# Edge convolutions of a graph network: TensorE picks the rows of 5 of 17 tiles with one-hot matrices, GpSimd gathers the other 12

## The reference

```python
def _egnn_conv(x, src, dst, edge_attr, W_msg, W_edge, W_root, b):
    msg = x[src] @ W_msg + edge_attr @ W_edge
    agg = jax.ops.segment_max(msg, dst, num_segments=x.shape[0])
    agg = jnp.where(jnp.isneginf(agg), 0.0, agg)
    return agg + x @ W_root + b
c1 = leaky_relu(_egnn_conv(X, ...1)); c2 = leaky_relu(_egnn_conv(c1, ...2))
x = _layernorm(x + c2)
```

## Time and profile before

| what | us |
|---|---|
| median of 3 runs | 3147.15 (3136.76 to 3154.84) |
| the profiled execution's own time | 3183.81 |
| its span, first to last instruction | 3181.8 |
| loop of layer 0, first sum to last maximum | 1910.6 to 2473.7 |
| loop of layer 1, to its last maximum | 2550.0 to 3119.4 |

### The profile page before, as it was taken

The page is one execution under the profiler, slowest core; times in us unless marked ns, Lnnn a source line. Parts: engine busy times, 40 slices in busy tenths (PEclk is TensorE's granted clock), DMA queues, the critical chain, the costliest instruction groups (busy, mean ns, idle before and its releaser), DMA issues. The chain is left out here.

```text
span 3181.8 us, 47118 instructions
## 1 busy us (share of the span) xinstructions
PE 2077.3 (65%) x15259; PEld 1621.9 (51%) x15259; DVE 1566.5 (49%) x5813; ACT 268.0 (8%) x521; POOL 1421.2 (45%) x1251
## 2 busy tenths in 40 slices
PE   2397566999999999968557954444444544444442
PEld 1132114999999999958453443333333433333331
DVE  7699897555555555554450043333333333333336
ACT  3175441000000000001100010000000000000000
POOL 0100005888888884000000026666666466666663
PEclk9855556999999999969688965555555555555555
DMA  0391001222222221000009612222222222222221
GB/s 24 119 408 66 1 1 1 3 2 3 3 3 2 3 3 2 2 4 1 4 1 361 242 40 75 77 82 77 76 80 74 59 75 75 79 77 81 76 76 51
DMA packets 139880, 197.83 MB, mean 62 GB/s; under 512 B 91361, under 2 KB 92929, under 8 KB 136082
## 3 DMA queue, kind: packets, MB, share of 16 engines
q0 software_dynamic: 83472, 42.24, 11.4%
q1 hardware_dynamic: 41394, 112.23, 9.6%
q10 hardware_dynamic: 14800, 40.59, 3.2%
HBM read 103.85 MB, written 91.10 MB: 61 GB/s over the span
## 5 line engine op out<-in xcount | busy, mean ns | idle before, releaser
L1049 POOL DMA_INDIRECT rows_c<-y_table,srci_sb x782 | 740.1, 946 | 632.1 <-issue 228.1
L1195 PE MATMUL ps<-w_edge,ea_c 32*128 32x96 f32 x1564 | 529.5, 466 | 609.8 <-DVE whole_messages_c L1108 365.9
L516 PE MATMUL ps<-parts,at 128*128 128x192 f16 x10000 | 836.6, 247 | 37.0 <-DVEq L578 20.2
L516 PEld LDWEIGHTS ps<-parts,at 128*128 128x128 f16 x10000 | 830.9, 98 | 42.8 <-issue 38.6
L1195 PEld LDWEIGHTS ps<-w_edge,ea_c 32*128 32x128 f32 x1564 | 384.2, 308 | 755.2 <-DVE whole_messages_c L1108 430.0
L553 POOL DMA_INDIRECT weight_matrix<-w,place x391 | 608.9, 1557 | 119.1 <-issue 119.1
L1108 DVE TENSOR_TENSOR whole_messages_c<-rows_c,ps 128x96 f32<-128x96 f32 x782 | 195.8, 254 | 511.5 <-issue 303.2
L1116 DVE SCALAR_TENSOR_TENSOR run_c<-run_c,brk,whole_messages_c 128x96 f32<-128x96 f32 x782 | 248.4, 318 | 225.2 <-issue 199.1
L506 PE MATMUL ps<-onekey,oneplace 128*128 128x200 f16 x784 | 271.0, 347 | 96.7 <-DVE oneplace L479 96.7
L588 DVE SCALAR_TENSOR_TENSOR t<-ps,coef,g 128x96 f32<-128x96 f32 x400 | 127.2, 318 | 313.0 <-PE ps L516 258.4
L506 PEld LDWEIGHTS ps<-onekey,oneplace 128*128 128x128 f16 x784 | 81.3, 104 | 286.6 <-DVE oneplace L479 286.6
(11 more groups left out here) (279 smaller groups left out, 1313.1 us busy)
## 6 DMA issues: line engine op xcount, KB each, us to landing
weight_matrix<-blank SPq DMA_DIRECT2D x28, 1600.0 KB, 19.7
weights<-weight_matrix SPq DMA_DIRECT2D x28, 1600.0 KB
run_max<-run_c ACTq DMA_DIRECT2D x48, 432.0 KB
run_max<-run_c ACTq DMA_DIRECT2D x48, 384.0 KB
rows_c<-y_table,srci_sb POOLq DMA_INDIRECT x782
ea_c<-in_eaT SPq DMA_DIRECT2D x46, 144.0 KB
weight_matrix<-w,place POOLq DMA_INDIRECT x391
ea_c<-in_eaT SPq DMA_DIRECT2D x46, 128.0 KB
```

What stands on the lines that cost most here:

```text
L516: mm = nc.tensor.matmul(m.ps[:, bank, 0:2 * D], m.at[:, s, blk * P:(blk + 1) * P], parts[:, s, :], start=(s == 0), stop=(s == NB - 1))
L1049: nc.gpsimd.indirect_dma_start(rows[:, t % TURN, :], None, d.yt, bass.IndirectOffsetOnAxis(m.srci[:, t:t + 1], 0)).then_inc(got[t % TURN], 16)
L1195: nc.tensor.matmul(m.ps[:, j % NBK, 0:D], ea[:, j, :], m.we[:, layer, :], start=True, stop=True).then_inc(msg, 1)
```

## The change

Tiles 0, 3, 6, 9 and 12 of each turn (`PICKED`) are no longer gathered. TensorE picks their rows out of the table itself: the table is scaled by a power of two and split into a high and a low f16 part (`parts`, 25 blocks of 128 x 192), and for each of the 25 node blocks b a one-hot matrix `hot[:, b, :]` (128 nodes x 640 edges, f16) says which of its nodes is the source of which edge. 25 x 5 matmuls of 192 columns accumulate in 5 PSUM banks, 5 more add the edge term, ScalarE copies the 5 pairs of parts out of PSUM (`take_rows`), and VectorE's sum of a picked tile adds the two parts.

The one-hots of a turn are made a turn or more ahead: 17 of the 25 blocks by VectorE (one comparison each), 8 by ScalarE (blocks 1, 4, ... 22; |source - node|, then Relu(1 - gap), two instructions each). Both read `srcb`, the 640 source numbers of a turn spread to all partitions by a transfer that ScalarE issues. There is one `srcb`: it is loaded for turn k+2 when all one-hots of turn k+1 are done. The edge terms of the other 12 tiles have 3 PSUM banks instead of 6. The maxima are now stored by SP. The table is stored in one transfer, after the scaling, in both layers at the start of the convolution; the scale needs the maximum over the table, which a reduction on GpSimd spreads.

```diff
+PICKED = (0, 3, 6, 9, 12)
+BY_ACT = tuple(range(1, NB, 3))
+BY_DVE = tuple(b for b in range(NB) if b not in BY_ACT)
+SPLIT_B = 13
 # GpSimd
+            g.wait_ge(mx, 1)
+            nc.gpsimd.partition_all_reduce(ga[:], gm[:], P, RMAX).then_inc(amx, 1)
+            g.wait_ge(yst, 16)
             for t in range(T):
+                if t % TURN in PICKED:
+                    continue
 # ScalarE
+            def load_sources(k):
+                of = sources[bass.ds(k * TURN, 3 * NPK), :].rearrange("(i s) e -> i s e", s=3)[:, 0, :]
+                a_.dma_start(srcb[:], of.unsqueeze(0).to_broadcast([P, NPK, P])).then_inc(srcl, 16)
+            def onehots(k, blocks):
+                for b in blocks:
...
+                    nc.scalar.activation(gap[:], srcb[:].rearrange("p i e -> p (i e)"), ACT.Abs,
+                                         bias=m.unshift[:, b:b + 1]).then_inc(gapd, 1)
+                    a_.wait_ge(gapd, len(BY_ACT) * k + (n + 1))
+                    nc.scalar.activation(hot[:, b, :], gap[:], ACT.Relu, bias=1.0, scale=-1.0).then_inc(hota, 1)
+                    a_.wait_ge(hota, len(BY_ACT) * k + (n + 1))
+            def take_rows(k):
+                a_.wait_ge(closed, k + 1)
...
+            with a_.Fori(0, TN - 2) as k:
+                onehots(k + 1, high)
+                a_.wait_ge(hotv, len(BY_DVE) * (k + 2))
+                load_sources(k + 2)
+                onehots(k + 2, low[:2])
+                take_rows(k + 1)
+                onehots(k + 2, low[2:])
 # VectorE
+            v.wait_ge(amx, 1)
+            scale_of(nc, do, m, ga[:], scl[:], un[:])
+            nc.vector.tensor_scalar(m.ytab[:], m.ytab[:], scl[:], None, ALU.mult).then_inc(scaled, 1)
...
+            do(nc.vector.tensor_copy(parts[:, :, 0:D], m.ytab[:]))
+            nc.vector.tensor_tensor(parts[:, :, D:2 * D], m.ytab[:], parts[:, :, 0:D], ALU.subtract).then_inc(split, 1)
+            onehots(0, BY_DVE)
+                        if j in PICKED:
+                            i = PICKED.index(j)
+                            v.wait_ge(picked, NPK * k + (i + 1))
+                            nc.vector.tensor_tensor(whole[:, j % 2, :], pairs[:, i, 0, :], pairs[:, i, 1, :],
+                                                    ALU.add).then_inc(summed, 1)
+                    if more and 1 <= j <= 8:
+                        onehots(k + 1, high[j - 1:j])
+                    if ahead and 9 <= j:
+                        onehots(k + 2, low[j - 9:j - 8])
 # TensorE
+            def turn(k, more):
+                for u, j in enumerate(REST):
+                    pe.wait_ge(summed, TURN * k + (TURN + REST[u - EB] + 1 if u >= EB else REST[u - EB] + 1))
+                    nc.tensor.matmul(m.ps[:, 5 + u % EB, 0:D], ea[:, j, :], m.we[:, layer, :], start=True,
+                                     stop=True).then_inc(msg, 1)
+                    if more:
+                        upto = min(NB, -(-(u + 1) * NB // NR))
+                        for b in range(done, upto):
+                            pick(k + 1, b)
```

More of the change, by code:

```diff
@@ L54 @@
 assert T % TURN == 0
+TN = T // TURN
+PICKED = (0, 3, 6, 9, 12)
+NPK = len(PICKED)
+PK = NPK * P
+MID = 1600
+BY_ACT = tuple(range(1, NB, 3))
+BY_DVE = tuple(b for b in range(NB) if b not in BY_ACT)
+SPLIT_B = 13
+REST = tuple(j for j in range(TURN) if j not in PICKED)
+NR = len(REST)
 EPS = 1e-5
@@ new lines, in take_rows @@
+            def take_rows(k):
+                a_.wait_ge(closed, k + 1)
+                if not (isinstance(k, int) and k == 0):
+                    a_.wait_ge(summed, TURN * k + (PICKED[-1] + 1))
+                for i, j in enumerate(PICKED):
+                    nc.scalar.activation(pairs[:, i, :, :].rearrange("p a f -> p (a f)"), m.ps[:, i, 0:2 * D],
+                                         ACT.Copy).then_inc(picked, 1)
+            low = [b for b in BY_ACT if b < SPLIT_B]
+            high = [b for b in BY_ACT if b >= SPLIT_B]
@@ L1077, in _ @@
+            onehots(TN - 1, high)
+            take_rows(TN - 1)
             if layer == 0:
@@ L1084, in _, with onehots @@
             do = Chain(v, chain)
+            def onehots(k, blocks):
+                for b in blocks:
+                    v.wait_ge(srcl, 16 * k + 16)
+                    if not (isinstance(k, int) and k == 0):
+                        v.wait_ge(used, NB * k + (b + 1 - NB))
+                    nc.vector.tensor_scalar(hot[:, b, :], srcb[:].rearrange("p i e -> p (i e)"), m.shift[:, b:b + 1],
+                                            None, ALU.is_equal).then_inc(hotv, 1)
             if layer == 0:
@@ L1099, in _ @@
                                             ALU.is_equal).then_inc(seld, 1)
+            low = [b for b in BY_DVE if b < SPLIT_B]
+            high = [b for b in BY_DVE if b >= SPLIT_B]
+            onehots(1, low)
             v.wait_ge(runz, 1)
@@ L1119, in _ @@
                         v.wait_ge(ran, TURN * k + (e + 1 + TURN))
+            with v.Fori(0, TN - 2) as k:
+                turn(k, True, True)
+            turn(TN - 2, True, False)
+            turn(TN - 1, False, False)
             v.wait_ge(lt, 1)
@@ L1186, in _ @@
             pe.wait_ge(rc, NG)
[L1188 to L1196 removed]
+            pe.wait_ge(split, 1)
@@ new lines, in _, with pick @@
+            pe.wait_ge(wscaled, 1)
+            def pick(k, b):
+                if b in BY_ACT:
+                    pe.wait_ge(hota, len(BY_ACT) * k + (BY_ACT.index(b) + 1))
+                else:
+                    pe.wait_ge(hotv, len(BY_DVE) * k + (BY_DVE.index(b) + 1))
+                if b == 0 and not (isinstance(k, int) and k == 0):
+                    pe.wait_ge(picked, NPK * k)
+                for i in range(NPK):
+                    one = hot[:, b, i * P:(i + 1) * P]
+                    mm = nc.tensor.matmul(m.ps[:, i, 0:2 * D], one, parts[:, b, :], start=(b == 0), stop=False)
+                mm.then_inc(used, 1)
+                if b == NB - 1:
+                    pe.wait_ge(eapl, 16 * k + 16)
+                    for i in range(NPK):
+                        mm = nc.tensor.matmul(m.ps[:, i, 0:D], eap[:, i, :], m.we[:, layer, :], start=False, stop=True)
+                    mm.then_inc(closed, 1)
@@ L1197, in _ @@
+            with pe.Fori(0, TN - 1) as k:
+                turn(k, True)
+            turn(TN - 1, False)
             pe.wait_ge(ran, T + TURN)
```

161 lines of the change are left out of this document (114 added, 47 removed).

## The result

The changed kernel takes 3283.84 us (median of 4 runs, 3272.09 to 3295.07). To the kernel before (3150.99 us, 4 runs) the ratio is 1.043, interval 1.038 to 1.048: slower, where I had forecast 3029 us. The time is outside my range (2925 to 3265).

The account below looks back on a forecast made before the run. It took gathers served at 1.42 us each to bound the 25.05 us turn. A new turn of 11.0 + 3.9 + 0.1 + 4.1 + 3.2 = 22.3 us saved 118 us over both layers: 3029 us, range 2925 to 3265.

Parts of the forecast that it names:

- What the change removes: Gathers in a turn: five of 17 go, GpSimd needs 15.0 us, the shared path 17.0 us, the late phase is gone.
- late phase: Later part of each turn in the kernel before: with GpSimd 6 or 7 gathers ahead, VectorE's rows wait 1.16 and 2.46 us.
- 1.42 us a gather: Pace at which something shared by gathers and other engines' waits serves gathers; 17 take 24.1 us of a 25.05 us turn.
- The source load: Mid-turn load of `srcb`: issued at 11.0 us, landing 3.9 us later, bounds 2.6 and 10.1; VectorE idles nearly 6 us.
- ScalarE's chain: ScalarE before the source load: copies 1.2 us, then six blocks of 1.64 us, 9.8 us; load issued at 11.0 us.
- TensorE: TensorE's work in a turn: 125 picks and 17 edge terms, 14.8 us at full clock or 28.5 at half.
- closing stretch: TensorE from the end of sum 13 to the next copies: 3.1 us at full clock, 5.5 at half, 3.2 taken.
- VectorE, ScalarE and the edges of the loops: One-hot 382 ns, ScalarE block 1.64 us; layer 0 starts at 1917 us, layer 1's sums 36 us into its stage.
- From the profiled execution to the median: Last step to the forecast time: median of the runs 36.7 us under the profiled execution, 3065.8 us becoming 3029.
- The second one: Rival: late phase stays as more semaphores are posted, VectorE loses most of 9 us; 28 us a turn, 3270 us, chance 0.12.
- The first rival: TensorE stays at 1.2 GHz through the loops: 28.5 us of work a turn, 3315 us; chance 0.11.
- my own bounds of 20.9 to 24.6: Range in us for the 22.3 us turn; 20.9 with a 2.6 us load and full clock, 24.6 without the load's worst case.

Follow-up runs that it names:

- e6: The changed kernel without its 12 gathers a turn, VectorE adding a row of the root product instead; 3108.52 us, 0.987 to the kernel before.
- c4: The changed kernel unedited, run again on another chip; 3284.77 us, 1.046 to the kernel before.
- e7: The changed kernel with GpSimd clearing a small tile behind each gather, so steps are 1.53 us instead of 1.25; 3195.13 us, 1.008 to the kernel before.
- e4: The kernel before with 12 of its 17 gathers a turn; 2676.59 us, 0.902 to the kernel before.
- e10: The changed kernel with two source buffers (low and high blocks loaded separately) and no gathers; 2976.41 us, 1.005 to the kernel before.
- e3: The changed kernel with two source buffers, one for low and one for high blocks, each loaded once its blocks are done; 2977.16 us, 1.002 to the kernel before.
- e1: The changed kernel with the gathers for slots 14, 15 and 16 held until TensorE has counted the closing terms; 3115.75 us, 1.051 to the kernel before.
- e2: The changed kernel with 40 idle matmuls on TensorE while it waits for the copies; 3087.62 us, 1.040 to the kernel before.
- c3: The changed kernel with the gathers for slots 14 to 16 held behind the closing terms, repeated on another chip; 3218.81 us, 1.011 to the kernel before.

## Why the prediction was wrong, step by step

- **What the change removes: wrong, and it is the largest step.** I wrote that VectorE's pace spaces the gathers to 1.34 us, "so I count the late phase as gone". It stayed: six gathers in a row, at steps of 1.25 to 1.7 us, made the count of the closing matmuls 3.4 us late in a steady turn. Without gathers 3.8 us of a turn and 176 us are gone (e6 against c4). My figure of 1.42 us a gather doesn't carry over: in the turns the lateness stays at 1.53 us (e7), and on other chips 1.25 us do no harm (e4). It holds only where 12 gathers run beside the first picks of a layer, where 1.53 us are slow enough.
- **The source load.** Its own time was right (3.9 forecast, 3.72 measured), and to wait for it costs 2.8 to 3.3 us a turn where nothing is late (e10 against e6, e3 against e1). When it is issued was wrong by 2.35 us. I counted ScalarE's chain (11.0 us; its last one-hot ends at 11.55) and VectorE "ready behind message 8, some 9 us into its turn", and left out that VectorE's messages hang on edge terms that TensorE does in order between two blocks each, at half clock 2.38 us a group.
- **TensorE.** I took half clock as a bound of the closing stretch (3.1 or 5.5 us; it took 2.7 at full clock) and didn't carry it into the first half, where it is spent. Its idle of 4.55 us ends with a clock of 0.50, and in the turn shown its first 45 picks and three edge terms take 9.5 us, where at the full clock's pace of the later rows they would take 5.4: some 4 us more. E2 against e1 has 3.6. The work itself I also had too small: 14.8 us a turn at the full clock, while the turn of e3 at 1.00 has TensorE busy for 17.4. An edge term is 0.39 us from start to start and not 0.24, a pick 0.093 and not 0.085. I had taken the edge term from matmuls of another shape. The Trainium skill (TensorE: Matmul & The Clock Gate, HAM oscillation) says that idle gaps within a loop throttle the clock anew each time; the trace agrees, with 0.50 at the start of the turn shown and 0.75 over the whole of it, and my sum should have had the half at the turn's start.
- **VectorE, ScalarE and the edges of the loops.** A one-hot was 382 ns forecast and is 380 without gathers beside it, 407 with them. ScalarE's block was 1.64 us and is 1.70 (the rows give 0.87 ns a column where I wrote 0.85). That layer 0 started at 1916.4 us where I said 1917 is in part luck, since three more profiles of this kernel have 1907 to 1922. Layer 1's start took 44.8 us instead of 36, and that is the late phase once more: it takes 33.6 us without gathers (e6) and 33.1 on a chip without the late phase (e1).
- **From the profiled execution to the median.** I carried over the 36.7 us between them from the kernel before, without a reason; they were -2.7.
- **The rivals.** The second one came true in kind and nearly in number: 28 us a turn and 3270 us, against 27.1 and 3284. It had a chance of 0.12. That the number is so near is luck, as it has neither the half clock nor the short work of TensorE, and it has the 36.7 us. Its place was another: I priced VectorE's rows, and it was TensorE's counts to ScalarE. What spoke against it in my text was that the propagation's transfers, 1.86 us apart, do no harm, but TensorE was dense there and hung on few counts. The first rival (half clock all through) isn't what happened. Without lateness the turn would have been 23.2 to 23.8 us (e6, e1), inside my own bounds of 20.9 to 24.6, and the time 3109 to 3116 us on chips where the kernel before has 3147 and 2970.

What stays open: what the gathers and the counts share; why a slower pace helps beside the first picks and not at the closing; what the changed kernel as it is takes on a chip without the late phase, where only e1 was run (1.051); why the same kernel settles at 27.1 us a turn on one chip and at 25.7 on another, both with the late phase; and what 12 gathers cost the kernel before on such a chip.

## What to carry to other kernels

If a wait appears in a profile that nothing visible ends, find out on which event it depends before pricing a change that leaves that event in place. Here the lateness followed the gathers to wherever they ran, and a loop that closes through one count (picks, copies, picks) pays for it in full each turn. A chain through two engines in program order is to be walked at the clock that the engine has after its idle stretch, not at the better one. And a difference to the kernel before holds for the chip it was run on; measure both beside each other, as here the same change was 1.1% and 4.6% slower on two chips. The kernel that an experiment edits belongs beside it as well: e1, e2 and e3 lacked the changed kernel, and so don't show what it takes on their chip.

## What the runs showed of the hardware

Chips differ in the late phase. Beside it goes a difference in the trace itself: of the 16 counts by which each of the 552 gathers reports, 8832 in all, the changed kernel's trace on the first chip holds some 4800, and that of e1 some 8800. On the page this is seen in the landing time, which can't be given for the first; the row of the changed kernel

```profile
rows_c<-y_table,srci_sb POOLq DMA_INDIRECT x552
```

and of e1:

```profile
rows_c<-y_table,srci_sb POOLq DMA_INDIRECT x552, 2.5
```

The same goes for the propagation: 1580 of its 6256 records on the first chip, 1587 in e6, which has no gathers in the loops, and all 6256 in e1 and e10. So it goes with the chip, or with the session on it, as no chip was visited twice, and not with the loop. In all six groups of runs, the first pair included, few records go with a kernel before of 3147 to 3182 us and nearly all records with one of 2962 or 2970. Whether lost records and late counts have one cause wasn't tried. Every run on record has a span and a granted clock and was thus recorded in some form, so these runs don't rule out that the recording itself makes the counts late on some chips.

The record of the closing count itself shows the two kinds of chip most plainly. In the middle turns it stands 0.01 us behind the last closing matmul in e1, e2, e3 and e10, and also in c3, where the gathers are held back, and in e6, where there are none. In the other runs it is 1.2 to 3.3 us on average.
